# A cross attention whose last sum of a head, maximum, shifts and late keys are put in another order

## The reference

```python
q = (inputs_q @ Wq).reshape(b, sq, H, HD) * (1.0 / np.sqrt(HD))   # H, HD = 16, 128
k = (inputs_kv @ Wk).reshape(b, skv, H, HD)
v = (inputs_kv @ Wv).reshape(b, skv, H, HD)
scores = jnp.einsum('bqhd,bkhd->bhqk', q, k)
attn = jax.nn.softmax(scores, axis=-1)
ctx = jnp.einsum('bhqk,bkhd->bqhd', attn, v).reshape(b, sq, H * HD)
return ctx @ Wo
```

## Time and profile before

| | us |
|---|---|
| median of 3 runs | 1643.83 (1641.98 to 1645.52) |
| the profiled execution, its own time | 1639.74 |
| its span, first to last instruction | 1637.7 |
| PE busy | 1597.1 (98%) |
| DVE busy | 1173.8 (72%) |
| ACT busy | 727.1 (44%) |
| POOL busy | 192.7 (12%) |

### The profile page before, as it was taken

How to read it: one execution, slowest core, us unless ns; L and a number is a source line. 1 busy time by engine, 2 the same in 40 slices (tenths; PEclk the granted TensorE clock), 3 DMA queues, 4 the chain that set the end, 5 groups by cost and what they waited for, 6 DMA issues and landing times.

```text
span 1637.7 us, 23093 instructions
## 1 busy us (share of the span) xinstructions
PE 1597.1 (98%) x8798; PEld 1255.4 (77%) x8798; DVE 1173.8 (72%) x2127; ACT 727.1 (44%) x981; POOL 192.7 (12%) x247
## 2 busy tenths in 40 slices
PE   9999999999999999999999999999999999999998
PEld 7888888888788888878888888887857757545454
DVE  5556888888788888878888889999583762633333
ACT  4334454555455455544555446555341361322221
POOL 0001011010101101011010101111100072011110
PEclk9999999999999999999999999999999999999999
DMA  7876555555555555555445443334421517489994
GB/s 237 228 230 195 155 144 135 149 155 139 156 156 142 139 152 147 141 168 142 123 128 141 130 129 116 102 105 128 149 82 49 205 52 296 189 254 414 424 423 173
DMA packets 125660, 283.48 MB, mean 173 GB/s; under 512 B 7728, under 2 KB 83696, under 8 KB 119408
## 3 DMA queue, kind: packets, MB, share of 16 engines
q1 hardware_dynamic: 103248, 201.27, 37.9%
q0 software_dynamic: 22304, 80.75, 17.3%
HBM read 207.51 MB, written 74.48 MB: 172 GB/s over the span
## 4 chain that ended last, share of the span: by engine, by line
PE 46%; issue 38%; DVE 8%; POOL 4%; ACT 2%; DMA 1%; POOLq 0%; SPq 0%; DVEq 0%; ACTq 0%
PE bank L41 10%; PE bank L503 9%; PE bank L471 6%; PE bank L2340 5%; POOL v_back L1191 2%; PE bank L2379 2%; PE bank L527 2%; PE bank L1906 2%; PE bank L2365 2%; PE bank L1920 1%; DVE e_parts L965 1%; DVE S L931 1%; POOL esum_t L1211 1%; PE bank L2369 1%; PE bank L526 1%
## 5 line engine op out<-in xcount | busy, mean ns | idle before, releaser
L503 PE MATMUL bank<-wv_parts,cT_hi 128*128 128x512 f32 x1024 | 334.4, 390 | 0.7 <-DMA wv_parts<-wv_dram 0.6
L503 PEld LDWEIGHTS bank<-wv_parts,cT_hi 128*128 128x128 f32 x1024 | 192.7, 188 | 41.5 <-DMA wv_parts<-wv_dram 1.1
L471 PE MATMUL bank<-cT_hi,wk_hi 128*128 128x512 f32 x512 | 200.9, 392 | 0.6 <-DVE cT_lo L859 0.6
L471 PE MATMUL bank<-cT_lo,wk_hi 128*128 128x512 f32 x512 | 199.8, 390 | 0.0
L503 PE MATMUL bank<-wv_parts,cT_lo 128*128 128x512 f32 x512 | 199.6, 390 | 0.0
L471 PE MATMUL bank<-cT_hi,wk_lo 128*128 128x512 f32 x512 | 199.5, 390 | 0.0
L705 ACT CAST e_parts<-S 128x1024 fp32r<-128x1024 f32 (+1 forms) x129 | 134.9, 1045 | 139.3 <-PE bank L527 133.4
L696 ACT ACTIVATE S<-S 128x1024 f32<-128x1024 f32 (+1 forms) x129 | 136.0, 1054 | 129.3 <-DVE S L931 128.0
L965 DVE TENSOR_TENSOR e_parts<-S,e_parts 128x1024 fp32r<-128x1024 f32 (+1 forms) x129 | 155.9, 1208 | 49.8 <-ACT e_parts L705 47.5
L882 DVE TENSOR_TENSOR mx<-mx,S 128x256 f32<-128x256 f32 x390 | 165.2, 424 | 32.4 <-ACT S L690 22.1
L931 DVE TENSOR_TENSOR S<-S,mrow 128x1024 f32<-128x1024 f32 (+1 forms) x129 | 157.9, 1232 | 4.8 <-POOL mrow L1204 4.8
(11 more groups left out here) (328 smaller groups left out, 2795.1 us busy)
## 6 DMA issues: line engine op xcount, KB each, us to landing
w<-in_w_moe SPq DMA_DIRECT2D x32, 2304.0 KB, 15.5
v_dram<-v_out SPq DMA_DIRECT2D x112, 512.0 KB, 4.5
v_back<-v_dram POOLq DMA_DIRECT2D x110, 512.0 KB, 4.6
ctx_nat<-in_ctx SPq DMA_DIRECT2D x8, 1024.0 KB, 5.4
ctx_raw<-in_ctxT SPq DMA_DIRECT2D x7, 1024.0 KB, 8.8
v_dram<-v_back SPq DMA_DIRECT2D x14, 512.0 KB, 4.7
v_late<-v_dram POOLq DMA_DIRECT2D x14, 512.0 KB, 3.6
wv_parts<-wv_dram POOLq DMA_DIRECT2D x6, 1024.0 KB, 8.0
```

Source lines behind the costliest of these rows:

```text
L471: t = e.matmul(banks[b][:], l, r, start=(c == 0 and m == 0), stop=(c == DT - 1 and m == 2))
L503: t = e.matmul(banks[b][:], l, r, start=(c == 0 and m == 0), stop=(c == DT - 1 and m == 2))
```

## The change

Six moves; no instruction is added or removed:

1. DVE, heads 0 to 11: the sum of chunk 7 (`sum_e(h, 7)`) stands ahead of the split of the next key weights, the maximum over chunk 6 and the values' split, and no longer behind them.
2. DVE, heads that don't start a quad: `shift(h, 0)` stands ahead of `split_k(h + 1, 0)`.
3. POOL, heads 4 and 8: `largest_score` stands ahead of `load_v`, and no longer behind it.
4. POOL: `add_sums` (the sum over partitions) waits until `shift(h + 1, 0)` is done.
5. DVE, heads 12 to 14: `shift(h, 2)` stands ahead of `sum_e(h, 1)`; `split_k(h + 1, 7)` ahead of the maximum over chunk 5 and of `split_e(h, 7)`; at head 12 the splits of `Wo` and of the result ahead of one maximum.
6. SP: the load of `Wo` stands at chunk 0 and no longer at chunk 2 (heads 1 to 14).

```diff
--- before.py
+++ after.py
@@ -420,8 +420,10 @@
                             e.wait_ge(q_projected, 2)
                             e.wait_ge(*v_spilled(KVT - 1))
                             load_qo(qo_order.index(("wq", 2)))
+                        elif h < XH - 1:
+                            e.wait_ge(q_projected, h + 2)
+                            load_qo(qo_order.index(("wo", h - 1)))
                         if h == XH - 2:
-                            e.wait_ge(q_projected, XH)
                             e.dma_start(x[:], a["x"]).then_inc(x_in, 16)
                         if not has_halves(h):
                             load_wk(h + 2)
@@ -432,9 +434,6 @@
                         load_wk(h + 2)
                     for u in units(h, j):
                         spill(u)
-                    if j == 2 and 0 < h < XH - 1:
-                        e.wait_ge(q_projected, h + 2)
-                        load_qo(qo_order.index(("wo", h - 1)))
                     if j == 5 and 0 < h < XH - 1:
                         e.wait_ge(y_projected, h)
                         load_qo(qo_order.index(("wq", h + 2) if h + 2 < XH else ("wo", h)))
@@ -1056,10 +1055,10 @@
                 split_q(h + 1)
                 if h and not starts_quad(h):
                     move_o(h - 1)
+                    shift(h, 0)
                 split_k(h + 1, 0)
-                if h:
+                if h and starts_quad(h):
                     shift(h, 0)
-                if h and starts_quad(h):
                     move_o(h - 1)
                 shift(h, 1)
                 if h:
@@ -1089,13 +1088,15 @@
                             shift(h, j + 1)
                         split_k(h + 1, j)
                     if j == NCH - 1:
+                        sum_e(h, j)
                         split_wk(h + 2)
                     keep_max(h + 1, j - 1)
                     for u in units(h, j):
                         split_v(u)
                     if j == 3 and h:
                         scale_o(h - 1)
-                    sum_e(h, j)
+                    if j < NCH - 1:
+                        sum_e(h, j)
                     if half_at(h, j) is not None:
                         split_half(half_at(h, j))
                     if j == 2 and h:
@@ -1115,26 +1116,26 @@
                 sum_e(h, 0)
                 split_k(h + 1, 1)
                 split_e(h, 1)
+                shift(h, 2)
                 sum_e(h, 1)
-                shift(h, 2)
                 for j in range(1, NCH):
                     if j + 2 < NCH:
                         shift(h, j + 2)
                     if j + 1 < NCH:
                         sum_e(h, j + 1)
-                    if j in (1, 3):
+                    if j in (1, 3, NCH - 2):
                         split_k(h + 1, j + 1)
+                    if j == 3 and h == LATE:
+                        split_qo("wo", h - 1)
+                        split_o(h - 1)
                     keep_max(h + 1, j - 1)
                     if j + 1 < NCH:
                         split_e(h, j + 1)
-                        if j not in (1, 3):
+                        if j not in (1, 3, NCH - 2):
                             split_k(h + 1, j + 1)
                     if j == 2:
                         invert_row(h - 1)
                         scale_o(h - 1)
-                    if j == 3 and h == LATE:
-                        split_qo("wo", h - 1)
-                        split_o(h - 1)
                     if j == 5 and h == XH - 2:
                         add_heads()
                     if j + 1 == NCH - 1 and h + 2 < XH:
@@ -1206,6 +1207,7 @@
             def add_sums(h):
                 if h:
                     e.wait_ge(scaled, h)
+                e.wait_ge(shifted, NCH * (h + 1) + 1)
                 if h < LATE:
                     e.wait_ge(e_summed, summed(h, NCH - 1))
                     e.partition_all_reduce(esum_t[:], esum[:], P, bass.bass_isa.ReduceOp.add).then_inc(sum_ready, 1)
@@ -1222,6 +1224,8 @@
                     if j == 0 and starts_quad(h) and h:
                         load_wv(h // HPQ + 1)
                     if h < LATE:
+                        if h and j == 0 and starts_quad(h):
+                            largest_score(h)
                         load_v(n)
                         if n == 0:
                             load_wv(1)
@@ -1237,7 +1241,7 @@
                         load_v(n + 1)
                     elif n + 3 < NH:
                         load_v(n + 3)
-                    if h and j == 0 and n != TAIL:
+                    if h and j == 0 and n != TAIL and not (h < LATE and starts_quad(h)):
                         largest_score(h)
                     if j == 0 and 0 < h <= LATE or j == 1 and LATE < h < XH - 1:
                         add_sums(h - 1)
```

## The result

Six runs of the changed kernel have a median of 1632.41 us (1632.21 to 1632.89), six of the kernel before 1642.9 (1641.35 to 1645.52): a ratio of 0.9935, 95% interval 0.9922 to 0.9948. The forecast, 1631.7, is 0.7 off. But its four terms don't all stand: in the two profiles three came out at least at their size, and the largest, the quads' 5.0 us, at nothing.

What follows compares the result with a forecast made beforehand. TensorE was taken to set the pace up to head 11, with VectorE having next to no slack from head 12. Terms 5.0 + 4.9 + 1.5 + 0.7 = 12.1 us off the 1643.83 median gave 1631.7 us, range 1627.5 to 1639.7.

Steps and rivals of the forecast that it cites:

- The nine heads (4.9): Heads 1 to 11 except 4 and 8: an earlier write speeds chunk 1's value load, ending PE's waits; 4.9 us saved.
- Quads (5.0): Starts of heads 4 and 8: earlier maximum and shorter shift cut PE's waits by 2.1 and 1.2, plus 1.7 of clock.
- I add that difference, 0.7, both times (bounds 0 and 1.4): Heads 4 and 8: Wo's load, 256 KB, joins the crowd and lengthens the value load by 0.7 us each time.
- the last unit's write: Under "At no cost": the values' split of a head's last unit comes later, but its write lands before its buffer is refilled.
- the 5.3: Head 8: the value load takes 5.3 us, with the next key weights (256 KB) issued into the same crowd.
- The gain of the clock: Head 4: with PE waiting only 1.1 us, no 0.50 clock stretch follows; 1.7 us gained, bounds 0 and 1.7.
- The other half of the chain: Head 4: shift ends about 419.5, so the rests are there at 423.1, at the latest 423.6; values then come last.
- the values come later still: Rival at the quads: loads take 1.4 longer and the clock falls, so 1.9 of 5.0 remain; 1634.8 us, chance 0.10.
- Head 12 (1.5): Start of head 12: shift loses 0.9 us by preceding POOL's sum, and the earlier maximum gives 0.6; 1.5 us saved.
- Heads 12 to 14 (0.7): DVE's 0.51 us wait for chunk 7's score copy goes twice, plus small ACT waits; 0.7 us, bounds -0.5 and 1.5.

Runs made afterwards that it cites:

- the load that waited for the write: Kernel before, nine heads: the load of chunk 1's values waits until the write of projected values in flight has landed; one execution, 1664.75 us.
- the run with the sum first: Kernel before with one edit, heads 0 to 11: sum of chunk 7 ahead of key weights' split, maximum over chunk 6 and values' split; 1643.51 us.
- the run with the sum free: Changed kernel without the wait of GpSimd's sum for the first shift, so the sum runs right behind the maximum; 1633.76 us, ratio 0.9949.
- the run in the old order: Changed kernel with heads 12 to 14 in the order of before on DVE; one execution, 1633.81 us.
- keys first: Changed kernel with the keys' split ahead of the first shift again in heads that start no quad; 1637.48 us, ratio 0.997.

## Why the prediction was right or wrong

- **The nine heads (4.9): right.** Lead 3.99 (forecast 3.9), load 3.6 in head 3 (forecast 3.4 to 3.7; 3.5 to 3.8 in the nine), all waits gone: 4.4 + 9 x 0.17 = 5.9, the upper bound. Only the two edits together do it, as the working had it, and the cause was tested by the load that waited for the write.
- **Quads (5.0): wrong, 0 in the two profiles.** The step that failed is "I add that difference, 0.7, both times (bounds 0 and 1.4)". The loads grew by 1.6 and 2.7 us. By the profiles compared Wo was 1.05 of it each time; the remainder was the last unit's write, which I had as harmless as long as its buffer came free (the run with the sum first shows it without Wo), and at head 8 the key weights, whose share I had taken as already in the 5.3. I priced one new transfer and left out that the others stood closer together. The gain of the clock hung on a short wait, and went with it. The other half of the chain held: the rests end 4.1 us behind the load's issue, forecast 4.2 to 4.7, and are hidden. The rival "the values come later still" was the true one, at 0.10, and even it left 1.9.
- **Head 12 (1.5): right.** The shift takes 1.23 us, and PE's excess there fell from 2.0 to 0.54. Both parts show by themselves: 0.9 in the run with the sum free, 0.6 in the one with the sum first.
- **Heads 12 to 14 (0.7): right in kind, too small:** 1.5 by the run in the old order, the upper bound.
- **Sum.** Held against each other at the issue of the same value load, the profile of after is 1.7 us behind at head 1 (207.45, before 205.78) and 4.5 ahead at head 12 (979.40, before 983.87). Between these it wins 6.1 in the nine heads and nothing at the quads: 2.5 are won from head 4 to head 5 and 2.5 lost from head 8 to head 9. From head 12 to the end it wins 2.9, half at the entry and half behind it. 6.1 + 0 + 2.9 - 1.7 = 7.3, as the spans differ. The 1.7 come before 170 us, among others in a wait of 1.8 us for keys at 160.8 (0.8 before). No instruction is moved there; with the hidden part it is 2.0 us, other runs with the same order lose 0.9 to 1.6 at that place, and the one with the sum first, nearly the kernel before, 2.0 as well, so most of it looks like scatter.
- **The median: met by luck.** It moved by 10.5, the profiles by 7.5: the profile of before lies 3.2 below the median of its six runs, that of after at its own median. I had carried the sum from the profile to the median as if the distance stayed. Most of it is the clock. Of 40 runs of the kernel before beside the experiments, the nine with a mean granted clock of 0.997, that of both profiles, took 1640.1 to 1642.0 us, and the six at 0.993 and 0.994 took 1643.0 to 1644.9; the runs of the changed kernel are all at 0.996 or 0.997. At 0.997 the means are 1640.7 and 1632.4: the change is worth about 8.3 at a like clock. The other 2 of the 10.5 are then time at the lower level that the usual run of before has more; the six runs behind the 10.5 themselves list no clock, and whether the change takes this time away no run shows. The forecast met the median because that distance, which I didn't price, covered most of what the quads failed to give.

## What to carry to other kernels

A transfer that looks free because its own consumer is far away is paid by the load whose consumer is near: before a load is moved, list what is in flight when the critical one is issued. Two edits that each gain nothing or lose can gain together when one makes the slack that the other spends, so test them alone and as a pair. And a time that is met doesn't confirm a sum: compare term by term.

## What the runs showed of the hardware

- POOL's sum, 1.79 us in its record, lets no subtraction of two SBUF inputs pass until about 0.95 us from its start: second shifts, 1.22 long where nothing holds them, that begin 0.35 us behind it (head 4) and 0.71 (head 3) both end 2.17 to 2.18 behind it.
- A load of 512 KB from HBM took 3.4 to 3.8 us with a write of 512 KB issued 4 us ahead, 3.5 to 4.2 with one issued 3 us ahead (the sum free), and 4.0 to 4.8 with one issued 2 us ahead. 256 KB more in the crowd at the quads cost it 1.05 us in the profiles compared, twice; over all profiles at head 4 it is 0.6 to 1.1 (5.8 to 6.2 us with Wo and the late write, 5.1 to 5.2 with the late write alone).
- TensorE's granted clock fell to 0.5 behind a wait of 1.89 us (head 4, keys first) and not behind 2.25 (head 4, changed kernel) or 3.25 (head 8, keys first); behind the waits of under 1.4 us at the quads it never fell. How long PE was idle doesn't settle it alone, and these runs don't show what does.
